# Decoder layer: score groups paired, the router's chain in later slots, and the scan's output broadcast by DMA

## The chip, the cores and the metric

The kernel runs on one core of one Trainium2 chip. The metric is the device time of one execution in microseconds, the median of repeated runs; lower is better. TensorE's clock is granted by the chip at 2.4 GHz (1.00 in the profile) or at half of it, 1.2 GHz (0.50).

## The reference

A decoder layer on 16 batches of 256 tokens with 256 dimensions, in float32, with three parts, each followed by a residual and a layer norm (`d`, `ctx` and the weights are inputs):

```
xh, gate = split(x @ W_in.T + b_in)               # 512 + 512
xh = silu(conv4(xh) + conv_b)
u  = xh @ W_ssm.T + b_ssm                         # 32 states
h_t = h_{t-1} @ A.T + u_t * Bv ; s_t = h_t @ Cv   # scan over the tokens: one number s per token
y  = (s + Dv) * xh * silu(gate)
x  = norm(x + (y @ W_out.T + b_out + x))
x  = norm(x + attention(q=x, k=v=ctx))            # 16 heads of 16
x  = norm(x + moe(x))                             # router softmax, best of 8 experts, 640 places each
```

The last layer norm and the expert sum run over 4096 tokens; a token beyond an expert's 640 places is passed through, so the router must count the tokens in order.

## The kernel before

`decoder` runs three blocks one after the other. `mixer_in` (L63) projects all tokens, convolves, and computes the scan as a few matmuls with precomputed powers of A; it leaves `gated` = xh * silu(gate) for all tokens in SBUF and the scan's output `s_all` (L370), [128 partitions x 64], in a folded layout. `attend` (L375) does everything from the mixer's output to the router for one batch after the other. `experts` (L1058) runs the eight experts.

`attend` is a software pipeline written out by hand. `run` (L455) calls `step(n, p)` of each engine for n from -1 to 19, the middle ones in a hardware loop. A step has 16 slots h. In step n the engines work on several batches at once: the mixer's output of batch n+1, the keys and queries of batch n, the first scores and the values of n-1, the second scores of n-2 and n-3, the output projection of n-3, the router of n-4. Each engine goes through its own step in program order and waits on semaphores; a wait holds all that stands behind it on that engine. The rows call a stretch of one step a batch here, from one first score group to the next.

TensorE (`step`, L780). `scores` (L702) forms query by key of one pair of heads with four matmuls of 48 rows, two on the lower and two on the upper half of the array (L711), into `ps_m`; VectorE takes the row maxima from there (L946), and the next group waits for that. After all eight groups `maxima_rows` (L695, L699) transposes the maxima, ScalarE copies them (`mrow`, L857), and SyncE sends them into `qst`. `scores_t` (L715, L721) forms key by query with the maxima subtracted, into `ps_a`; ScalarE takes the exponential into `pt` (L903), and the next group waits for that. `weigh` (L725, L736) multiplies four heads with the values. There is one buffer of `ps_m` and one of `ps_a`. `scores` stands in even slots, `scores_t` AL = 3 slots behind, so in odd ones.

The dense matmuls take turns on one PSUM bank `ps_d`: `spread_s` (slot 12, L644), `mixer_out` (14 and 15, L670), `keys` (1 and 2), the transposes of `x1` (5), `queries` (7, L689), `values` (9 and 10). The bank `ps_e` goes round among `maxima_rows` (0), the transposes of `pay` (1), `router` (2), `count` (6), `sums_by_query` (7 and 9, L741), the transposes of `onrm` (11), `project_out` (12 and 13, L751).

How s gets to y before the change: VectorE lays s of one batch on the diagonal of `diag` (slot 7, L1044), `spread_s` multiplies it with a matrix of ones, which leaves s of all 256 tokens on all 128 partitions in `ps_d`, and VectorE forms `y` = (s + Dv) * gated from PSUM (slot 13, L1050).

VectorE (`step`, L937), slots: 0: row maximum, `r1` (L951, the residual of the mixer from `ps_d`), `pay` (L959, the norm after attention of batch n-4), the statistics of `r1`; 1: mean and variance, `ve1`; 2: statistics of `pay`; 3: `x1` (L977), `ve3`, the logits `lg` (L986) and their maximum; 4: the negated maximum `ntop` (L994), the index, the one-hot rows `hot` (L1000); 6 to 9: place in the expert, `dest`; 8 and 10: `onrm` (L1029); 14: `r2` (L1035, the residual of attention from `ps_e`) and its statistics; 15: `ve2`.

ScalarE (L851): the exponentials, the copies out of PSUM, `kq` with bias (slots 3 and 8), the high halves of keys and queries (`half`, slots 4 and 9). GpSimd (POOL, L587): powers for the norms, the low halves (L583), `twice` (L609), `x2b` and the scatter of the rows. SyncE (L526) stores the halves to DRAM and reads them back stacked into `kst` and `qst` (`store`, `stack`, L500): keys and queries of batch n must be back before the first scores of step n+1. Its queue is one order too.

## Time and profile before

| | |
|---|---|
| median of 3 runs | 1017.29 us (1015.42 to 1017.44) |
| the profiled execution | 1020.84 us, its span 1019.1 us |
| busy over the span | TensorE 85%, its weight loads 65%, VectorE 59%, ScalarE 40%, GpSimd 35% |
| mean granted clock | 0.909 |
| `mixer_in` / `attend` / `experts` begin at | 0 / 141.0 / 739.1 us |
| row maximum (L946), exponential (L903), mean of 128 | 1.224, 1.025 us |
| memset of `kst` on GpSimd, from 141.18 (L568) | 7.24 us |
| issue of one transfer on SyncE (at 142.19) | 0.38 us |

The profile is one execution; its own time is 3.55 us over the median. A row of a timeline gives the start, the duration of a run of like instructions, engine, line, operation and tiles, their number, and in brackets the idle time of the engine before it and what ended that. Starts of successive rows are the safer measure, since the ends of matmuls are modelled and overlap.

### The profile page before, as it was taken

The page shows a single profiled execution, that of the slowest core. Times are in us where ns is not written, and L with a number is a line of the kernel's source. Part 1 is how long each engine was busy: PE and PEld are TensorE (multiplying, and loading weights), DVE is VectorE, ACT ScalarE, POOL GpSimd, SP SyncE. Part 2 cuts the span into 40 slices and gives each one's busy share as a digit, 9 for nine tenths or more (in the row PEclk, how much of TensorE's full clock was granted, in tenths as well). Part 3 has the DMA queues.
Part 4 walks back from the last instruction along what each step waited for, and adds up shares of the span by engine and source line. Part 5 has one row for each costly group of instructions (what it writes and reads, how often), then busy time and mean ns, then how long its engine had stood idle before and what let it go on. Part 6 is the DMA issues. An engine that isn't in the chain of part 4 may idle for free. (4 is left out here: it accounts for less than half of the span.)

```text
span 1019.1 us, 16854 instructions
## 1 busy us (share of the span) xinstructions
PE 863.1 (85%) x5964; PEld 663.5 (65%) x5964; DVE 597.7 (59%) x1441; ACT 405.0 (40%) x623; POOL 354.1 (35%) x290
## 2 busy tenths in 40 slices
PE   5998947789899888988989888887279999999993
PEld 4776725455666566655666556544279999999993
DVE  4889751545675777667676666643235555555542
ACT  4565611145444444445444454443043334233320
POOL 0333352222233434344342443223212442244422
PEclk9999967679998999999999998877579999999997
DMA  3117302444443445444344442400343222343100
GB/s 115 42 43 210 108 24 78 113 106 126 104 126 115 109 111 125 124 113 114 103 124 121 117 114 74 116 21 24 106 135 109 94 88 90 113 128 106 46 22 22
DMA packets 73432, 98.82 MB, mean 97 GB/s; under 512 B 10529, under 2 KB 60874, under 8 KB 73376
## 3 DMA queue, kind: packets, MB, share of 16 engines
q1 hardware_dynamic: 69920, 89.95, 32.0%
q0 software_dynamic: 3456, 8.13, 2.2%
q8 instruction: 34, 0.56, 0.2%
q14 instruction: 22, 0.18, 0.1%
HBM read 63.40 MB, written 35.73 MB: 97 GB/s over the span
## 5 line engine op out<-in xcount | busy, mean ns | idle before, releaser
L946 DVE TENSOR_REDUCE nmax<-ps_m 128x4 f32<-128x1024 f32 x128 | 156.6, 1224 | 174.6 <-PE ps_m L711 172.1
L903 ACT ACTIVATE pt<-ps_a 128x1024 f32<-128x1024 f32 x128 | 131.1, 1025 | 89.7 <-PE ps_a L721 88.3
L1216 ACT ACTIVATE hid<-ps_h 128x640 fp32r<-128x640 f32 x64 | 45.1, 705 | 151.3 <-PE ps_h L1156 151.3
L1156 PE MATMUL ps_h<-xt,w_hi 128*128 128x320 f32 x512 | 99.9, 318 | 1.0 <-DVE xt L1231 1.0
L1168 PE MATMUL ps_y<-w_hi,hid 128*128 128x256 f32 x640 | 85.3, 284 | 1.7 <-issue 1.7
L1265 DVE SCALAR_TENSOR_TENSOR hid<-ps_h,hid 128x640 fp32r<-128x640 f32 x64 | 52.7, 824 | 56.2 <-ACT hid L1216 55.7
L1156 PEld LDWEIGHTS ps_h<-xt,w_hi 128*128 128x128 f32 x512 | 80.0, 191 | 5.5 <-DVE hid L1265 3.9
L1168 PEld LDWEIGHTS ps_y<-w_hi,hid 128*128 128x128 f32 x640 | 80.1, 192 | 1.9 <-issue 1.9
L721 PE MATMUL ps_a<-qst,kst 49*128 49x256 f32 x512 | 67.8, 345 | 15.5 <-ACT pt L903 15.2
L721 PEld LDWEIGHTS ps_a<-qst,kst 49*128 49x128 f32 x512 | 40.8, 197 | 57.0 <-issue 31.8
L711 PE MATMUL ps_m<-kst,qst 48*128 48x256 f32 x512 | 66.9, 342 | 11.1 <-DVE nmax L946 5.9
L736 PE MATMUL ps_o<-pt,vals 128*32 128x256 f32 x1024 | 74.6, 412 | 0.0
L340 DVE SCALAR_TENSOR_TENSOR conv<-ps_xh,taps,conv 128x510 f32<-128x510 f32 (+2 forms) x96 | 71.7, 747 | 3.4
L158 POOL TENSOR_TENSOR gated<-xh,sgate 128x512 f32<-128x512 f32 x32 | 42.3, 1320 | 90.3 <-ACT xh L245 90.3
L674 PE MATMUL ps_d<-w_out_sb,y 128*128 128x256 f32 x256 | 66.8, 409 | 5.2 <-DVE y L1050 5.2
L1312 POOL DMA_INDIRECT out_rows<-gated,token x40 | 39.4, 985 | 84.1 <-issue 84.1
L711 PEld LDWEIGHTS ps_m<-kst,qst 48*128 48x128 f32 x512 | 41.5, 200 | 39.9 <-issue 23.1
L583 POOL TENSOR_TENSOR half<-kq,half 128x512 fp32r<-128x512 f32 x32 | 40.6, 1268 | 73.0 <-ACT half L841 73.0
L674 PEld LDWEIGHTS ps_d<-w_out_sb,y 128*128 128x128 f32 x256 | 49.0, 201 | 16.3 <-DVE y L1050 6.7
L1156 PE MATMUL ps_h<-xt,w_lo 128*128 128x320 f32 x256 | 58.9, 312 | 0.0
L1279 DVE SCALAR_TENSOR_TENSOR gated<-ps_y,gated 128x256 f32<-128x256 f32 x40 | 19.3, 483 | 64.8 <-PE ps_y L1168 64.8
L1300 POOL TENSOR_TENSOR w_lo<-gated,w_hi 128x2048 fp32r<-128x2048 f32 x8 | 47.4, 5923 | 27.1 <-ACT w_hi L1206 27.1
(169 smaller groups left out, 1654.9 us busy)
## 6 DMA issues: line engine op xcount, KB each, us to landing
halves_dram<-half SPq DMA_DIRECT2D x64, 256.0 KB, 2.4
gated<-in_w SPq DMA_DIRECT2D x16, 1024.0 KB, 5.4
kst<-halves_dram SPq DMA_DIRECT2D x64, 128.0 KB, 3.1
qst<-halves_dram SPq DMA_DIRECT2D x64, 128.0 KB, 3.2
rows_dram<-blank SPq DMA_DIRECT2D x1, 5160.0 KB, 19.7
gated<-rows_dram SPq DMA_DIRECT2D x8, 645.0 KB, 4.2
x_raw<-in_x_t SPq DMA_DIRECT2D x8, 512.0 KB, 3.9
xres<-in_x SPq DMA_DIRECT2D x16, 256.0 KB, 3.6
```

What stands on the lines that cost most here:

```text
L340: op = nc.vector.scalar_tensor_tensor(out[:, :, late:S], ps[:, :, 0:S - late], taps[:, m, k:k + 1], out[:, :, late:S], ALU.mult, ALU.add)
L674: mm = pe.matmul(ps_d[:, t * D:(t + 1) * D], y[:, m, t * P:(t + 1) * P], w["out"][:, m, :], start=(m == 0), stop=(m == MH - 1), skip_group ...
L711: mm = pe.matmul(ps_m[:, side, t, :], qst[base:base + MR, p, k, t * P:(t + 1) * P], kst[base:base + MR, p, k, :], start=True, stop=True, s ...
L721: mm = pe.matmul(ps_a[:, side, t, :], kst[base:base + MR + 1, p, k, t * P:(t + 1) * P], qst[base:base + MR + 1, p, k, :], start=True, stop ...
L736: mm = pe.matmul(ps_o[VW * i:VW * (i + 1), g, :], vals[:, p, t, h, :], pt[:, h // 2 % 4, h % 2, t, :], start=(t == 0), stop=(t == KT - 1), ...
L903: nc.scalar.activation(pt[:, k % 4].rearrange("p s t q -> p (s t q)"), ps_a[:].rearrange("p s t q -> p (s t q)"), ACT.Exp).then_inc(s["exp ...
L946: nc.vector.tensor_reduce(nmax[:, q, :, :, h // 2].rearrange("p t s -> p s t"), ps_m[:], AX.X, ALU.max, negate=True).then_inc(s["max_done" ...
L1156: mm = pe.matmul(ps_h[:, f % 2, c2, 0:HC], w1[a][:, p, k, f * P:(f + 1) * P], xt[:, b, p, k, c2 * HC:(c2 + 1) * HC], start=(n == 0 and k = ...
L1168: mm = pe.matmul(ps_y[:, (p + t) % 2, 0:D], hid[:, a, f, t * P:(t + 1) * P], w2[b][:, p, f, :], start=(n == 0 and f == 0), stop=(n == 2 an ...
L1216: nc.scalar.activation(hid[:, HI, f, :].rearrange("p (c n) -> p c n", c=2), ps_h[:, f % 2, :, 0:HC], ACT.Relu).then_inc(s["hid_hi"], 1)
L1265: nc.vector.scalar_tensor_tensor(hid[:, LO, f, :].rearrange("p (c n) -> p c n", c=2), ps_h[:, f % 2, :, 0:HC], 0.0, hid[:, HI, f, :].rearr ...
L1300: nc.gpsimd.tensor_tensor(flat(w2[LO][:, p]), flat(w2_raw), flat(w2[HI][:, p]).bitcast(F32), ALU.subtract).then_inc(s["w2_lo"], 1)
```

## The change

Five things. `AL` goes from 3 to 4, so that a group of `scores` and a group of `scores_t` stand one behind the other in each even slot, and the other work of TensorE follows them; `weigh` moves ahead of the dense work of its slot. The dense work gets new slots: `mixer_out` 11 and 13, `values` 8 and 9, `sums_by_query` 8 and 10, the transposes of `onrm` 12, `project_out` both halves in 14. The router's chain moves back: transposes of `pay` 2, `router` 4, `lg` to `hot` 5, `count` 7, the rest a slot later; the statistics of `r1` come before `pay`, `r2` goes to slot 15, and `ntop` is made by ScalarE. `diag`, `spread_s` and the mask go: at the end of `mixer_in` TensorE transposes `s_all`, VectorE copies it, and SyncE writes it in four transfers to DRAM; `load_s` reads one batch's 256 numbers repeated over 128 partitions into `sb`, two batches ahead, and `y` (slot 6) is formed from it. The waits for `v_out` and `q_out` that stood in `spread_s` stand in `mixer_out`. Declarations of tiles and semaphores are left out here.

```diff
@@ -147,6 +149,12 @@
             sp.dma_start(dram["rows"].rearrange("(t p) r -> p t r", p=P),
                          c["blank"][:, None, :].to_broadcast([P, E * CAP // P, ROW])).then_inc(c["rows_blank"], 16)
 
+            sp.wait_ge(st_ready, 1)
+            for cq in range(4):
+                sp.dma_start(dram["scan"].rearrange("b (q c i) -> q b c i", q=4, c=4)[cq],
+                             c["s_rows"][B * cq:B * (cq + 1), :].rearrange("p (c n) -> p c n", c=4)[:, :, 0:L]
+                             ).then_inc(c["scan_out"], 16)
+
         @block.gpsimd
         def _(pool):
@@ -226,6 +234,12 @@
                                ends[:, 0:4 - lag, :].rearrange("p c b -> p (c b)"),
                                start=False, stop=(lag == 3), skip_group_check=True)
             mm.then_inc(s_mm, 1)
+
+            pe.wait_ge(s_ready, 1)
+            pe.wait_ge(gate_ready, MH * NG)
+            pe.wait_ge(c["loaded"], 16 * len(c["loads"]))
+            pe.transpose(ps_gate[0:4 * B, 0, 0:P], s_all[:].rearrange("p c b -> p (c b)"), c["eye"][:]
+                         ).then_inc(st_mm, 1)
 
         @block.scalar
@@ -368,7 +382,9 @@
             last.then_inc(ends_ready, 1)
             dve.wait_ge(s_mm, 1)
             nc.vector.tensor_copy(s_all[:], ps_xh[:, 0, 0:4 * B].rearrange("p (c b) -> p c b", b=B)).then_inc(s_ready, 1)
-            dve.wait_ge(s_ready, 1)
+            dve.wait_ge(st_mm, 1)
+            nc.vector.tensor_copy(c["s_rows"][:], ps_gate[0:4 * B, 0, 0:P]).then_inc(st_ready, 1)
+            dve.wait_ge(st_ready, 1)
@@ -381,22 +397,22 @@
...
-    AL, WL = 3, 5
+    AL, WL = 4, 5
@@ -496,6 +513,11 @@
...
+
+            def load_s(j, p):
+                settled(sp)
+                need(sp, s["y_done"], j - 1)
+                sp.dma_start(sb[:, p], dram["scan"][bass.ds(j, 1), :].to_broadcast([P, S])).then_inc(s_in[p], 16)
...
+            sp.wait_ge(c["scan_out"], 64)
+            load_s(0, 0)
             load_x(0, 0)
             load_ctx(0, 0)
 
             def step(n, p):
+                if on(n, -2):
+                    load_s(n + 2, p)
@@ -641,13 +667,6 @@
...
-            def spread_s(j):
-                pe.wait_ge(s["diag_done"], j + 1)
-                need(pe, s["v_out"], j - 1)
-                need(pe, s["q_out"], j)
-                pe.matmul(ps_d[:, 0:S], ones[:], diag[:].rearrange("p c i -> p (c i)"), start=True, stop=True
-                          ).then_inc(s["sbc_mm"], 1)
@@ -670,6 +689,8 @@
             def mixer_out(j, t):
                 if t == 0:
                     pe.wait_ge(s["y_done"], j + 1)
+                    need(pe, s["v_out"], j - 1)
+                    need(pe, s["q_out"], j)
@@ -782,45 +803,46 @@
                 for h in range(NH):
                     if h % 2 == 0 and on(n, 1):
                         scores(n - 1, q, h // 2)
-                    if h == 0 and on(n, 2):
-                        maxima_rows(n - 2, p)
                     j, head, lag = behind(n, h, AL)
                     if head % 2 == 0 and on(n, lag):
                         scores_t(j, p if lag == 2 else q, head // 2)
-                    if h == 12 and on(n, -1):
-                        spread_s(n + 1)
-                    if h in (14, 15) and on(n, -1):
-                        mixer_out(n + 1, h - 14)
-                    if h in (1, 2) and on(n, 0):
-                        keys(n, p, h - 1)
+                    if h == 0 and on(n, 2):
+                        maxima_rows(n - 2, p)
+                    j, head, lag = behind(n, h, WL)
+                    if head % PV == PV - 1 and on(n, lag):
+                        weigh(j, p if lag == 2 else q, head // PV)
+                    if h == 1 and on(n, 0):
+                        keys(n, p, 0)
+                    if h == 2 and on(n, 4):
+                        pe.wait_ge(s["x2_done"], n - 3)
+                        if on(n, 2):
+                            pe.wait_ge(s["m_out"], n - 1)
+                        turn(ps_e, pay[:, p], s["x2t_mm"])
+                    if h == 2 and on(n, 0):
+                        keys(n, p, 1)
+                    if h == 4 and on(n, 4):
+                        router(n - 4)
                     if h == 5 and on(n, 0):
                         pe.wait_ge(s["k_out"], n + 1)
                         pe.wait_ge(s["x1_done"], n + 1)
                         turn(ps_d, x1, s["x1t_mm"])
+                    if h == 7 and on(n, 4):
+                        count(n - 4)
                     if h == 7 and on(n, 0):
                         queries(n, 0)
                         queries(n, 1)
-                    if h in (9, 10) and on(n, 1):
-                        values(n - 1, q, h - 9, n if on(n, 0) else None)
-                    if h == 6 and on(n, 4):
-                        count(n - 4)
-                    if h in (7, 9) and on(n, 3):
-                        sums_by_query(n - 3, (h - 7) // 2)
-                    if h == 11 and on(n, 3):
+                    if h in (8, 10) and on(n, 3):
+                        sums_by_query(n - 3, (h - 8) // 2)
+                    if h in (8, 9) and on(n, 1):
+                        values(n - 1, q, h - 8, n if on(n, 0) else None)
+                    if h == 12 and on(n, 3):
                         pe.wait_ge(s["on_done"], 2 * (n - 3) + 2)
                         turn(ps_e, onrm, s["ont_mm"])
-                    if h in (12, 13) and on(n, 3):
-                        project_out(n - 3, h - 12)
-                    if h == 1 and on(n, 4):
-                        pe.wait_ge(s["x2_done"], n - 3)
-                        if on(n, 2):
-                            pe.wait_ge(s["m_out"], n - 1)
-                        turn(ps_e, pay[:, p], s["x2t_mm"])
-                    if h == 2 and on(n, 4):
-                        router(n - 4)
-                    j, head, lag = behind(n, h, WL)
-                    if head % PV == PV - 1 and on(n, lag):
-                        weigh(j, p if lag == 2 else q, head // PV)
+                    if h in (11, 13) and on(n, -1):
+                        mixer_out(n + 1, (h - 11) // 2)
+                    if h == 14 and on(n, 3):
+                        project_out(n - 3, 0)
+                        project_out(n - 3, 1)
@@ -859,7 +881,13 @@
...
-                    if h == 5 and on(n, 4):
+                    if h == 6 and on(n, 0):
+                        act.wait_ge(s["x1t_mm"], n + 1)
+                        nc.scalar.copy(x1t[:].rearrange("p k t -> p (k t)"), ps_d[:]).then_inc(s["x1t_out"], 1)
+                    if h == 6 and on(n, 4):
+                        act.wait_ge(s["top_out"], n - 3)
+                        nc.scalar.mul(ntop[:], top[:, :, 0], -1.0).then_inc(s["ntop_out"], 1)
+                    if h == 7 and on(n, 4):
                         j = n - 4
                         act.wait_ge(s["ntop_out"], j + 1)
                         need(act, s["pay_ready"], j)
...
-                    if h == 6 and on(n, 0):
-                        act.wait_ge(s["x1t_mm"], n + 1)
-                        nc.scalar.copy(x1t[:].rearrange("p k t -> p (k t)"), ps_d[:]).then_inc(s["x1t_out"], 1)
...
-                    if h == 12 and on(n, 3):
+                    if h == 13 and on(n, 3):
...
-                    if h == 11 and on(n, 1):
+                    if h == 10 and on(n, 1):
...
-                    if h == 2 and on(n, 4):
-                        act.wait_ge(s["x2t_mm"], n - 3)
-                        nc.scalar.copy(x2t[:].rearrange("p k t -> p (k t)"), ps_e[:]).then_inc(s["x2t_out"], 1)
...
+                    if h == 2 and on(n, 4):
+                        act.wait_ge(s["x2t_mm"], n - 3)
+                        nc.scalar.copy(x2t[:].rearrange("p k t -> p (k t)"), ps_e[:]).then_inc(s["x2t_out"], 1)
@@ -951,7 +976,13 @@
...
-                    if h == 0 and on(n, 4):
+                    if h == 0 and on(n, 0):
+                        dve.wait_ge(s["r1_done"], n + 1)
+                        stats(st1, r1, s["stats1"])
+                    if h == 1 and on(n, 0):
+                        mean_var(dc, st1, mv1, s["stats1"], n)
+                        nc.vector.tensor_scalar(ve1[:], mv1[:, :, 1], EPS, None, ALU.add).then_inc(s["var1_ready"], 1)
+                    if h == 1 and on(n, 4):
                         dve.wait_ge(s["rstd2"], i + 1)
...
-                    if h == 0 and on(n, 0):
-                        dve.wait_ge(s["r1_done"], n + 1)
-                        stats(st1, r1, s["stats1"])
-                    if h == 1 and on(n, 0):
-                        mean_var(dc, st1, mv1, s["stats1"], n)
-                        nc.vector.tensor_scalar(ve1[:], mv1[:, :, 1], EPS, None, ALU.add).then_inc(s["var1_ready"], 1)
...
-                    if h == 3 and on(n, 4):
+                    if h == 5 and on(n, 4):
+                        need(dve, s["ntop_out"], i)
                         dve.wait_ge(s["logit_mm"], i + 1)
                         nc.vector.tensor_copy(lg[:].rearrange("p t e -> p (t e)"), ps_e[:, 0:KT * E]).then_inc(s["lg_out"], 1)
                         dve.wait_ge(s["vo_row"], 1)
...
-                    if h == 4 and on(n, 4):
+                    if h == 5 and on(n, 4):
+                        dve.wait_ge(s["vo_row"], 1)
                         dve.wait_ge(s["top_out"], i + 1)
-                        nc.vector.tensor_scalar(ntop[:], top[:, :, 0], -1.0, None, ALU.mult).then_inc(s["ntop_out"], 1)
...
-                    if h == 6 and on(n, 4):
...
-                    if h == 7 and on(n, 4):
...
-                    if h == 8 and on(n, 4):
...
-                    if h == 9 and on(n, 4):
...
-                    if h in (8, 10) and on(n, 3):
-                        t = (h - 8) // 2
+                    if h in (9, 11) and on(n, 3):
+                        t = (h - 9) // 2
...
-                    if h == 14 and on(n, 3):
+                    if h == 15 and on(n, 3):
...
-                    if h == 7 and on(n, -1):
-                        need(dve, s["sbc_mm"], n + 1)
-                        nc.vector.tensor_tensor(diag[:], s_all[:, :, bass.ds(n + 1, 1)].to_broadcast([P, 4, 64]),
-                                                mask[:, None, :].to_broadcast([P, 4, 64]), ALU.mult
-                                                ).then_inc(s["diag_done"], 1)
-                    if h == 13 and on(n, -1):
-                        dve.wait_ge(s["sbc_mm"], n + 2)
+                    if h == 6 and on(n, -1):
+                        dve.wait_ge(s_in[q], use(n + 1, 16, q))
+                        need(dve, s["wout_mm"], n + 1)
                         for m in range(MH):
-                            op = nc.vector.scalar_tensor_tensor(y[:, m, :], ps_d[:, 0:S], c["d_col"][:, m:m + 1],
+                            op = nc.vector.scalar_tensor_tensor(y[:, m, :], sb[:, q], c["d_col"][:, m:m + 1],
                                                                 gated[:, m, bass.ds((n + 1) * S, S)], ALU.add, ALU.mult)
                         op.then_inc(s["y_done"], 1)
```

## Rows read from the trace of the kernel before

**Rows 1.** Busy times by stretch: length, five engines' busy, PEclk, DMA share, GB/s.

```profile
264.21:617.20 352.99, 317.83 (x2346) 215.56 (x2344) 241.57 (x649) 165.46 (x275) 142.81 (x132) 0.96 0.43 115
...
296.60:329.98 33.38, 30.28 (x216) 20.71 (x214) 21.64 (x59) 15.02 (x25) 12.99 (x12) 0.90 0.40 112
...
362.56:393.52 30.96, 27.66 (x215) 18.73 (x213) 22.16 (x59) 15.06 (x25) 12.96 (x12) 1.00 0.45 120
393.52:425.43 31.91, 29.04 (x216) 19.72 (x214) 21.47 (x59) 15.05 (x25) 12.95 (x12) 0.95 0.45 116
```

**Rows 2.** Waits of TensorE from 264.21 to 616.9: us in total, times, longest.

```profile
PE ps_e L774 <- DVE hot L1000: 11.9, 11, 1.3
PE ps_a L721 <- ACT pt L903: 10.0, 11, 1.0
```

**Rows 3.** The same columns as rows 1, a stretch at half clock.

```profile
341.90:345.30 3.40, 3.40 (x12) 2.68 (x9) 0.56 (x3) 1.07 (x2) 0.64 (x1) 0.50 0.02 6
```

**Rows 4.** Timeline of TensorE in the batch from 362.56.

```profile
362.56 0.39 PE L699 MATMUL ps_e<-eye,nmax 128*16 128x128 f32 x2
...
364.64 1.10 PE L656 MATMUL ps_d<-ctx,w_k_sb 128*128 128x256 f32 x4 [0.26 <-DVE r L951]
...
368.40 0.50 PE L721 MATMUL ps_a<-qst,kst 49*128 49x256 f32 x4
368.74 0.40 PE L711 MATMUL ps_m<-kst,qst 48*128 48x256 f32 x4
369.06 1.07 PE L736 MATMUL ps_o<-pt,vals 128*32 128x256 f32 x16
370.10 0.50 PE L721 MATMUL ps_a<-qst,kst 49*128 49x256 f32 x4
370.53 0.66 PE L682 MATMUL ps_d<-eye,x 128*128 128x128 f32 x4
...
374.56 1.99 PE L689 MATMUL ps_d<-x1t,w_q_sb 128*128 128x256 f32 x8
...
384.38 0.70 PE L648 MATMUL ps_d<-diag,ones_sb 128*128 128x256 f32 x2
384.92 1.03 PE L755 MATMUL ps_e<-w_o_sb,ont 128*128 128x256 f32 x4
```

**Rows 5.** Timeline of VectorE in the same batch.

```profile
363.82 0.68 DVE L951 TENSOR_TENSOR r<-ps_d,x2b 128x512 f32<-128x512 f32 x1
...
369.44 0.17 DVE L986 COPY lg<-ps_e 128x16 f32<-128x16 f32 x1
...
369.87 1.21 DVE L946 TENSOR_REDUCE nmax<-ps_m 128x4 f32<-128x1024 f32 x1
370.99 0.94 DVE L994 TENSOR_SCALAR ntop<-top 128x2 f32<-128x2 f32 x1
...
372.44 0.36 DVE L1000 TENSOR_SCALAR hot<-kinds_sb,expert 128x8 bf16<-128x8 f32 x2
...
390.06 0.68 DVE L1035 TENSOR_TENSOR r<-ps_e,gated 128x512 f32<-128x512 f32 x1
...
391.91 0.17 DVE L1041 TENSOR_SCALAR ve<-mv 128x2 f32<-128x2 f32 x1
```

**Rows 6.** Timeline of TensorE in an early batch, where the transfers are waited for.

```profile
220.94 2.71 PE L689 MATMUL ps_d<-x1t,w_q_sb 128*128 128x256 f32 x8
...
236.54 0.50 PE L711 MATMUL ps_m<-kst,qst 48*128 48x256 f32 x4 [0.47 <-DMA qst<-halves_dram]
```

**Rows 7.** Timeline of POOL and of VectorE in the batch of rows 4.

```profile
372.74 2.44 POOL L609 TENSOR_SCALAR twice<-pay,mv,ve 128x256 f32<-128x256 f32 x2 [0.18 <-POOL ve L605]
...
374.68 0.43 DVE L1044 TENSOR_TENSOR diag<-s_all,mask_sb 128x256 f32<-128x256 f32 x1
```

**Rows 8.** Timeline of all engines as attention begins.

```profile
149.03 1.00 DVE L1044 TENSOR_TENSOR diag<-s_all,mask_sb 128x256 f32<-128x256 f32 x1
...
151.41 1.66 DVE L1050 SCALAR_TENSOR_TENSOR y<-ps_d,d_col_sb,gated 128x256 f32<-128x256 f32 x4 [1.38 <-PE ps_d L648]
```

28 lines of the change are left out of this document (16 added, 12 removed).

## The prediction

> **What bounds the kernel now.** I began with the table of time and profile: TensorE is busy 85% of the span, VectorE 59%, so I looked for the stretch where TensorE's order sets the pace. That is the middle stage, attention with the mixer's output and the router riding along. The view by stretches [rows 1] shows 11 alike batches in 352.99 us, 32.09 each. Three of the 11 run wholly at the granted clock of 1.00 (2.4 GHz) and take about 30.96, of which TensorE is busy 27.66 and idle 3.30. The other eight hold a spell at 1.2 GHz (mean 0.95, once 0.90) and take 31.9 to 33.4 [rows 1]. The waits of TensorE over the same batches [rows 2] say where the idle time comes from: the router's chain on VectorE (`hot`, 11.9 us in 11 batches), and right behind it the exponential on ScalarE (10.0). The spell at 1.2 GHz starts just after these two waits: one is seen at 341.9 [rows 3].
>
> The timeline of TensorE [rows 4] gives prices. A score group alone holds the engine from 370.10 to 370.53, 0.43 us. Two groups back to back hold it from 368.40 to 369.06, 0.66, not 0.86: a saving of 0.20 a pair. `spread_s` holds it 0.53 (384.38 to 384.92).
>
> **What the change does to a batch.** I walk from T, the start of the first score group, at full clock.
>
> Removed. `spread_s`: -0.53. Pairing: 16 groups stood in 15 places (one pair exists, the one just read), now in 8: 7 new pairs at 0.20, -1.40. On VectorE `diag` (0.43) and the negated maximum go; the latter was held 0.94 at 370.99 [rows 5] behind a POOL operation, though its work is small. On ScalarE the same negation comes in, a small instruction before an exponential that has not yet been asked for: nothing, or 0.3 if that cover is gone. Of the old 3.30 idle I take all out and put in the new waits:
>
> (1) The residual `r2` now runs in slot 15, after both halves of `project_out`, which end with the batch. TensorE's maxima transposes wait for it: 0.68 of DVE [rows 5], 0.12 to start and 0.14 to hand over (`r1` ends at 364.50, the keys start at 364.64 [rows 4, 5]) make T+0.94, against a pair that ends at T+0.66. New wait 0.28.
>
> (2) The keys wait for `r1`. On VectorE `r2` to `ve2` takes 390.06 to 392.08, 2.02; then the max reduce, 1.14 to the next start; then `r1`, 0.68 [rows 5]. Before, the `r2` chain ran under the last matmuls. Now it starts only after them, so the keys start at T + 0.12 + 2.02 + 1.14 + 0.68 + 0.14 = T+4.10. TensorE has until then a pair, the maxima (0.39 with its tail, 0.32 net) and a weigh group (1.00 net) [rows 4], and is free at T+2.26. New wait 1.84, the largest one, in place of 0.26. Moving `mixer_out` forward to slots 11 and 13 does not help: its sum has long been there when VectorE is free to read it.
>
> (3) The normalised rows `pay` now stand after `stats1` and `ve1`. Their transposes wait about 0.15 more; if POOL's power on `ve1` holds VectorE off, up to 0.85.
>
> (4) The router's logits are read after the third reduce. From `r1` to `lg` was 5.62 [rows 5]; with a reduce ahead of it T+3.28+5.62+1.14 = T+10.0, and the router itself ends at T+10.2 by TensorE's order. From `lg` to `hot` took 3.36, of which the reduce was 1.12 (369.87 to 370.99) and the held negation 0.94 less 0.09 of overlap [rows 5]: 1.39 left, so `hot` is ready at T+11.6 and the count starts at T+11.75. TensorE comes there at T+11.45 with nothing late. Wait 0.3, or 0.6 with one small operation held; I take 0.45.
>
> The waits of the later slots (`onrm`, `ont`) go: between each producer and its reader there is now a `mixer_out` half (1.9) or the values. Full-clock batch: 30.96 - 0.53 - 1.40 - 3.30 + (0.28 + 1.84 + 0.15 + 0.45) = 28.45 us.
>
> **The queries' way through DRAM.** The next batch's first scores wait for transfers that start with the queries. In an early batch the chain was bare: the queries end at 223.65, the scores start at 236.54 on their arrival, 12.9 us [rows 6]. The change puts one exponential (1.02, in the table) between the bias and the high half: 13.9. The queries end at T+13.9 (count 0.2, queries 1.99 [rows 4]), so the data land at T+27.8, 0.7 before TensorE. If they are late by up to 1.6 the keys' wait of (2) absorbs it. SyncE's queue gets a scan load at the head of a step, 0.4 of issue where it idles. Price 0.
>
> **The clock.** What the old waits cost in clock is 32.09 - 30.96 = 1.13 a batch, 1.0 to 1.7 in a batch that has a spell. The new waits (1) and (2) are 2.1 us of idleness with 1.3 of work between them; the old pair, 11.9 + 10.0 over 11 batches [rows 2], was 2.0 with 0.2 of work between. I expect a spell in nearly every batch and take 1.5, so 29.95. Per batch -2.1, over 11 batches -23.
>
> **`y` from SBUF.** `y` now reads two SBUF tensors and falls beside POOL's `twice`. In the rows `diag`, which also reads two, took 0.43 inside `twice` (374.68 in 372.74 to 375.18), but 1.00 beside a POOL operation with two inputs at 149.03 [rows 7, 8]. I take 0, since the neighbour is `twice`; bounds 0 to 1.2, half of `twice`. The Trainium skill ("SBUF — State Buffer", section Who interferes with whom) says that a VectorE instruction with two SBUF inputs contends with any GpSimd instruction that reads SBUF and that the later one fully blocks. By that rule `diag` at 374.68 would have waited and `y` would wait: the trace agrees at 149.03 and not at 374.68.
>
> **The edges.** Before attention: a transpose, a copy, four transfers. If all engines wait for the four issues (0.38 each, in the table) the stage starts 1.7 to 2.3 later, with POOL's memset of 7.24 (in the table) on the path; against it `diag` and `spread_s` no longer stand between 149.03 and `y` at 151.41 [rows 8]: -2.4. Sum 0, bounds -2 to +3. The scan's own way through DRAM hides under the memset. The batch before the 11 gains some 2, the first with exponentials may lose 1, the last steps without keys gain 1 and the drain loses 1, where the last weigh group is now ahead of the router. Together -1.
>
> **Sum:** -23 - 1 = -24 on the profiled execution's 1020.84, 996.8; that execution stands 3.55 over the median of the runs shown, so the forecast is 993.
>
> **Rivals.**
> A, the clock holds: the wait (2) is one piece, and in three batches of eleven waits of this size cost no clock. Then 28.45 a batch, -3.64 x 11 = -40, with the edges -41: 976. Against: the new wait is as long as the old two. Chance 0.12.
> B, half the gain or less: reduce and exponential of the groups before now both stand in front of one place, the second group of a pair sometimes waits, and pairing saves 0.7, not 1.4; (3) and (4) take their upper ends, 0.85 more. Then 28.45 + 1.55 + 1.5 = 31.5, -0.6 a batch, -7 with the edges: 1010. Against: at 368.40 a pair ran without a wait. Chance 0.12.
> C, `y` is held by `twice` each batch: `sums_by_query` waits for the place behind it, 0.6 to 1.2 on 11 batches: 1000 to 1006. Chance 0.08, since `diag` ran through. The rule of the Trainium skill on "SBUF — State Buffer", named above, makes this the outcome.
> D, slower: the clock stays at 1.2 GHz from the keys' wait through the keys, turn and router, because every wait there feeds the next. The 28.45 batch becomes the old 32.09 when 3.6 us are lost to the clock, that is 7.3 us at 1.2 GHz, a mean of 0.89. In one batch 0.90 is seen. With 10 us it is 33.5: +15, 1032. Chance 0.06.
> E, the two sides cancel, within 0.2% of before: 0.04.
> The forecast, 984 to 1001, keeps 0.58. A measurement of this kernel tells about 0.2% (2 us) from no change. Faster is forecast, A, B and C: 0.90; same 0.04; slower 0.06. The range 976 to 1010 reaches to A and to B and takes in C and the upper ends of (3), (4) and the prologue.
>
> **What would show it.** In the profile after: batches of 29.5 to 30.5; a wait of the keys on `r1` near 1.8 as TensorE's largest, one of the maxima on `r2` of 0.3, that on `hot` under 0.6, those on `onrm` gone; adjacent L711 and L721 groups at 0.66; `r2` directly after `project_out`. Wrong if the keys wait under 0.5, if the first scores wait for DMA over 1.6, if the mean clock of the batches is under 0.90 or all at 1.00.

## The result, and the profile after

| | before | after |
|---|---|---|
| median, us | 1016.36 (4 runs) | 975.67 (4 runs, 973.87 to 978.80) |
| ratio | | 0.9611, 95% interval 0.9571 to 0.9652 |
| profiled execution, us (span) | 1020.84 (1019.1) | 973.87 (972.1) |
| granted clock, 11 batches | 0.96 | 0.98 |

The change takes 3.9% off. (Ratios, here and below, leave disturbed runs out, so one can differ from the quotient of two medians, most for the first set with statistics in front, where two of four runs are left out.) 975.67 is 17 us under the forecast of 993 and 0.3 under the low end of the range. Taken as a ratio, so that the kernel before of the same set counts, it lies just inside: 976 on 1017.29 is 0.959, and 0.961 was measured. The medians differ by 40.7 us and the two profiled executions by 47.0, since the one of before is 4.5 over its median and the one after 1.8 under; 6.3 us of the table below are of that kind. It divides up the 47.0 (a batch begins with its maxima transposes, L699 before and L720 after):

| stretch | before | after |
|---|---|---|
| mixer, up to `s_all` | 140.29 | 137.46 |
| start of attention, first batches | 67.61 | 68.39 |
| the next two | 29.08, 27.23 | 29.85, 28.20 |
| the 11 alike batches | 352.99 | 316.09 |
| the last two steps | 30.75, 28.52 | 27.71, 23.83 |
| drain | 62.61 | 62.97 |
| experts | 280.0 | 277.6 |

So 36.9 of the 47.0 us lie in the 11 batches. This is the view by stretches of the kernel after, for all 11, for one batch at full clock and for one with a spell at 1.2 GHz, in the columns of [rows 1]:

```profile
263.90:579.99 316.09, 279.90 (x2321) 197.93 (x2321) 238.60 (x633) 164.46 (x286) 144.70 (x132) 0.98 0.49 132
...
292.78:320.34 27.56, 24.90 (x213) 17.60 (x211) 20.68 (x56) 14.99 (x26) 13.02 (x12) 1.00 0.46 135
320.34:350.16 29.82, 26.43 (x213) 18.71 (x212) 22.01 (x58) 14.99 (x26) 13.11 (x12) 0.94 0.46 129
```

A batch takes 28.74 on average. TensorE's work at full clock is about 24.85, its idle time (316.09 - 279.90) / 11 = 3.29, and the rest, 0.60, is work done at the lower clock. Before it was 27.66 + 3.20 + 1.23 = 32.09. Of the 3.35 us that a batch gains, 2.81 are therefore work that TensorE no longer does and 0.63 work that it no longer does at the lower clock; it waits as long as before. Four of the 11 batches hold a spell, where it was eight of 11 [rows 1].

The waits of TensorE over these batches of the kernel after (us in total, times, longest):

```profile
PE ps_d L675 <- DVE r L976: 16.0, 11, 2.0
PE ps_m L732 <- DMA qst<-halves_dram: 8.3, 11, 1.5
PE ps_e L795 <- DVE hot L1026: 8.0, 11, 0.9
PE ps_e L703 <- DVE pay L990: 2.6, 9, 0.4
PE ps_m L732 <- DVE nmax L971: 1.0, 3, 0.3
PE ps_e L720 <- DVE r L1061: 0.2, 1, 0.2
```

The waits for the exponential of [rows 2] and for `onrm` are gone, and that for `hot` fell from 11.9 to 8.0. The largest is now the keys' wait for `r1`. One that I had priced at nothing, the first scores' wait for their transfers, comes second.

The timeline of TensorE of the kernel after, across the edge of a batch:

```profile
349.49 0.51 PE L732 MATMUL ps_m<-kst,qst 48*128 48x256 f32 x4 [0.55 <-DMA qst<-halves_dram]
349.83 0.40 PE L742 MATMUL ps_a<-qst,kst 49*128 49x256 f32 x4
350.16 0.39 PE L720 MATMUL ps_e<-eye,nmax 128*16 128x128 f32 x2
350.48 1.07 PE L757 MATMUL ps_o<-pt,vals 128*32 128x256 f32 x16
353.03 1.10 PE L675 MATMUL ps_d<-ctx,w_k_sb 128*128 128x256 f32 x4 [1.48 <-DVE r L976]
...
355.03 0.66 PE L703 MATMUL ps_e<-eye,pay 128*128 128x128 f32 x4 [0.23 <-DVE pay L990]
...
360.97 0.18 PE L795 MATMUL ps_e<-hot,tri 128*128 128x8 bf16 x1 [0.60 <-DVE hot L1026]
...
365.18 1.89 PE L684 MATMUL ps_d<-w_v_sb,ctx 128*128 128x256 f32 x8
367.00 0.50 PE L732 MATMUL ps_m<-kst,qst 48*128 48x256 f32 x4
```

And the timeline of VectorE of the kernel after in the same batch, with one row of POOL (at 361.04) that stands beside `y`:

```profile
349.09 0.69 DVE L1061 TENSOR_TENSOR r<-ps_e,gated 128x512 f32<-128x512 f32 x1 [1.04 <-PE ps_e L776]
349.82 0.75 DVE L952 BATCH_NORM_STATS2 st<-r 128x6 f32<-128x256 f32 x2
...
351.06 1.23 DVE L971 TENSOR_REDUCE nmax<-ps_m 128x4 f32<-128x1024 f32 x1
352.20 0.68 DVE L976 TENSOR_TENSOR r<-ps_d,x2b 128x512 f32<-128x512 f32 x1
...
359.32 0.17 DVE L1012 COPY lg<-ps_e 128x16 f32<-128x16 f32 x1 [0.34 <-PE ps_e L785]
...
360.55 0.36 DVE L1026 TENSOR_SCALAR hot<-kinds_sb,expert 128x8 bf16<-128x8 f32 x2
...
361.04 2.69 POOL L635 TENSOR_SCALAR twice<-pay,mv,ve 128x256 f32<-128x256 f32 x2 [0.18 <-POOL ve L631]
...
362.25 1.89 DVE L1072 SCALAR_TENSOR_TENSOR y<-sb,d_col_sb,gated 128x256 f32<-128x256 f32 x4
...
365.53 1.22 DVE L1041 TENSOR_SCALAR over<-place 128x2 f32<-128x2 f32 x1
```

Read the two together. From T = 349.49 the pair takes until 350.16, 0.67 as forecast. The keys start at T+3.54, not T+4.10: `r2` already began at T-0.40, since it waits for the projection and not for the scores, while the scores themselves were held 0.55 by the transfer. From `r2` at 349.09 to `hot` at 360.55 VectorE has one gap above 0.2 us, the 0.34 ahead of `lg`. In that stretch TensorE waits three times (1.48, 0.23, 0.60).

### The profile page after: what moved, and what is told of

Its sections match the earlier page's. It is cut to its first block and busy times, and to the rows that moved or that the text cites. A ratio compares the mean times of both kernels' runs of the same rounds, so it can differ in the third digit from the quotient of the medians.

```text
span 972.1 us, 16867 instructions
## 1 busy us (share of the span) xinstructions
PE 805.2 (83%) x5933; PEld 635.1 (65%) x5933; DVE 594.3 (61%) x1410; ACT 404.9 (42%) x639; POOL 356.3 (37%) x290
## 5 line engine op out<-in xcount | busy, mean ns | idle before, releaser
L695 PE MATMUL ps_d<-w_out_sb,y 128*128 128x256 f32 x256 | 62.1, 388 | 11.1 <-DVE y L1072 9.8
L675 PE MATMUL ps_d<-ctx,w_k_sb 128*128 128x256 f32 x128 | 42.6, 466 | 21.1 <-DVE r L976 21.1
L646 POOL DMA_INDIRECT rows_dram<-pay,dest x32 | 33.2, 1036 | 64.0 <-DVE dest L1047 50.0
```

What stands on the lines that cost most here:

```text
L675: mm = pe.matmul(ps_d[:, m * S:(m + 1) * S], w["k"][:, k, m * P:(m + 1) * P], ctx[:, p, k, :], start=(k == 0), stop=(k == KD - 1), skip_gr ...
L695: mm = pe.matmul(ps_d[:, t * D:(t + 1) * D], y[:, m, t * P:(t + 1) * P], w["out"][:, m, :], start=(m == 0), stop=(m == MH - 1), skip_group ...
```

## The experiments

Times are medians, beside runs of the kernel before on the same chip. "Batches" is the same stretch of 11 in the profiled execution, and "TensorE idle" its idle time there. One execution can lie off its median: pairing alone was profiled at 999.01 us (7.3 over), all but the pairing at 984.33 (4.3 under), the early projection at 956.19 (5.8 under), the wait on `sel` at 955.85 (4.6 over).

| kernel | time | ratio to before (95%) | batches | TensorE idle |
|---|---|---|---|---|
| before | | | 352.99 | 35.2 |
| scan alone | 1015.30 | 1.0006 (0.9984 to 1.0027) | 352.59 | 37.7 |
| pairing alone | 991.73 | 0.9744 (0.9722 to 0.9767) | 333.81 | 29.9 |
| all but the pairing | 988.66 | 0.9729 (0.9713 to 0.9745) | 323.65 | 25.1 |
| the change | 975.67 | 0.9611 (0.9571 to 0.9652) | 316.09 | 36.2 |
| statistics in slot 12 | 976.82 | 0.9615 (0.9587 to 0.9642) | 317.27 | 36.1 |
| statistics in front, first set | 988.89 | 0.9659 (0.9574 to 0.9744) | 328.78 | 40.9 |
| statistics in front, second set | 983.15 | 0.9668 (0.9624 to 0.9713) | 321.66 | 40.6 |
| r1 first | 979.07 | 0.9636 (0.9603 to 0.9669) | 317.16 | 35.8 |
| q's split first | 976.90 | 0.9622 (0.9573 to 0.9671) | 322.21 | 32.5 |
| early projection | 961.96 | 0.9479 (0.9436 to 0.9521) | 301.00 | 22.1 |
| both of these | 954.96 | 0.9404 (0.9373 to 0.9435) | 299.85 | 19.4 |
| and a late count | 953.82 | 0.9377 (0.9340 to 0.9414) | 300.51 | 24.6 |
| and a wait on `sel` | 951.25 | 0.9298 (0.9254 to 0.9341) | 292.63 | 16.1 |

### The parts of the change by themselves

**Pairing alone**, on the kernel before:

```diff
-    AL, WL = 3, 5
+    AL, WL = 4, 5
```

> The kernel before with AL = 4 and nothing else: the two score groups share an even slot, all other work keeps its old slot. Theory S (a change between score groups and full-array matmuls costs TensorE some 0.1 us each way, and seven fewer of both make about 2 us less busy time a batch): TensorE's busy time per batch falls from 27.7 to about 25.7 to 26.3 at full clock, and some of it comes back as longer waits for hot, whose chain on VectorE has not moved: 10 to 22 us faster. Theory W (the gain came from the waits that the new slots took away and from the clock that they cost): busy time falls by at most 1.4 a batch and the waits take nearly all of it: within 5 us of before.

**All of the change but the pairing**, on the kernel after:

```diff
-    AL, WL = 4, 5
+    AL, WL = 3, 5
```

> The changed kernel with AL = 3: all new slots, the transfers for the scan, but score groups in alternate slots again. Theory S: 2 us more TensorE time in each of some 13 batches, partly under the waits for r1: 18 to 30 us slower than the changed kernel. Theory W: under 10 us slower.

**The scan by transfers alone**, on the kernel before, with `y` in its old slot and the slots of the router and projections as they were:

```diff
-            def spread_s(j):
...
+            def load_s(j, p):
+                settled(sp)
+                need(sp, s["y_done"], j - 1)
+                sp.dma_start(sb[:, p], dram["scan"][bass.ds(j, 1), :].to_broadcast([P, S])).then_inc(s_in[p], 16)
...
-                            op = nc.vector.scalar_tensor_tensor(y[:, m, :], ps_d[:, 0:S], c["d_col"][:, m:m + 1],
+                            op = nc.vector.scalar_tensor_tensor(y[:, m, :], sb[:, q], c["d_col"][:, m:m + 1],
```

> The kernel before with the scan's output repeated by transfers alone; diag and spread_s go, y is formed in slot 13 from sb, all else in its old slot. Both theories: 0.53 us of TensorE and 0.43 of VectorE less in 16 batches, and 1.5 to 2.5 us more before attention begins: 3 to 7 us faster. If the transfers for it disturb those of the scores, no gain or a loss.

What was measured: the view by stretches, of each kernel one batch that ran wholly at the full clock (of pairing alone the only one). First pairing alone:

```profile
442.75:471.48 28.73, 26.15 (x215) 18.45 (x214) 22.46 (x59) 15.03 (x25) 13.00 (x12) 1.00 0.50 129
```

All but the pairing:

```profile
355.57:384.34 28.77, 26.69 (x211) 17.99 (x211) 21.09 (x58) 14.90 (x27) 13.22 (x12) 1.00 0.50 134
```

The scan alone:

```profile
486.81:517.64 30.83, 27.29 (x213) 18.34 (x211) 22.20 (x58) 15.05 (x25) 12.94 (x12) 1.00 0.48 124
```

The second number is TensorE's work, 27.66 before. Pairing takes off 27.66 - 26.15 = 1.51 in the old order, and 26.69 - 24.85 = 1.84 in the new one. The scan takes off 0.37. All but the pairing takes off 0.97, so by difference the new slots bring some 0.6 of work, where I had none. The scan alone leaves the time as it was, where both theories had it 3 to 7 us faster: its idle time grows from 35.2 to 37.7, which is the 0.37 x 11 put back in two thirds (the copy `ont`, 2.7 in 11 batches, is waited for once `spread_s` no longer stands in front of its reader).

In time, pairing is worth 24 alone and 13 on top of the slots; the slots with the scan are worth 27 alone and about 16 on top of the pairing. Theory W falls on the kernel before, where the work fell by more than its 1.4 and the time by far more than its 5 us; theory S has the work right (26.15) and the time 2 to 4 us short. On top of the slots neither range holds: 13 lies between the "under 10" of W and the 18 to 30 of S. The two halves do not add up, since together they run into waits: idle time is 29.9 with the one, 25.1 with the other, and 36.2 with both. Against all but the pairing, the change waits 8.0 for `hot` where that kernel waits 0.8, and 8.3 for the load of the scores where that kernel has none; the keys' wait is nearly the same in both (16.0 and 15.5).

### What the front of the batch is bound by

**r1 first**: the statistics of `r2` and their mean move from the end of slot 15 to behind `r1`, on VectorE.

```diff
+                    if h == 0 and on(n, 4):
+                        dve.wait_ge(s["r2_done"], i + 1)
+                        stats(st2, c["r2"], s["stats2"])
...
                     if h == 15 and on(n, 3):
...
-                        dve.wait_ge(s["r2_done"], j + 1)
-                        stats(st2, c["r2"], s["stats2"])
```

> The changed kernel with the statistics of r2 (stats2, mean_var, ve2) moved behind r1 on VectorE, so that the keys wait no longer for them. Theory K (the chain project_out, r2, statistics, reduce, r1, keys sets the batch): the keys' wait falls from 1.45 to some 0.3, the batch from 28.7 to about 27.4: 12 to 16 us faster. Theory Q (the transfers that start with the queries and end at the next first scores are a second bound of nearly the same length, as the wait of 0.75 for them hints): the batch is a loop through keys, queries and transfers, and since the keys start earlier the transfers do as well: also faster, with the DMA wait larger than 0.75. If instead the wait for r1 was free because of the transfers: within 3 us of the changed kernel.

The waits of TensorE in that kernel:

```profile
PE ps_e L703 <- DVE pay L997: 14.4, 11, 1.4
PE ps_m L732 <- DMA qst<-halves_dram: 8.5, 11, 1.1
...
PE ps_d L675 <- DVE r L976: 4.5, 11, 0.5
```

The keys' wait fell from 16.0 to 4.5, that for `pay` rose from 2.6 to 14.4, and the batches stayed (317.16 for 316.09). The load's wait did not move either. Theories K and Q are wrong by their 12 to 16 us; the third reading has the time nearly right (within 3 us; 3.4 measured, with intervals that overlap) but not its reason, the transfers. The theory that describes it, called V from here: whichever instruction of TensorE's is in front, it meets VectorE's stretch from `r2` to `hot`; moving one instruction inside the stretch only moves the wait.

**Two more statistics per batch**, of a constant, into a tile that nobody reads: once behind `r1`'s own statistics in the stretch, once in slot 12.

```diff
+                        for t in range(KT):
+                            nc.vector.bn_stats(st_x[:, t, :], c["b_o"][:, 0:D])
```

> The changed kernel with two more batch statistics per batch on VectorE, of a constant, into a tile that nobody reads, put right behind the statistics of r1 (slot 0). By the rows of the changed kernel such a pair takes about 0.7 us. Theory V (the first third of a batch is VectorE's: its instructions run back to back from r2's drain to hot, and TensorE's waits there are that one stretch seen at several places): each of the 11 batches is longer by about 0.7, TensorE's waits for keys, pay and hot grow by that sum, and the time is 982 to 985 us. Rival M (the stretch of VectorE merely lies beside TensorE's, and the wait for the scores' load at the batch's edge takes up what comes late): below 3 us, 975 to 978 us.

> The same two statistics per batch, but in slot 12, where VectorE is idle. It adds the same work to VectorE's busy sum (about 0.7 us a batch), and the instruction order elsewhere is unchanged. Theory V: within 1 us of the changed kernel, 974 to 977 us, since only what lies between r2's drain and hot counts. Rival W (VectorE's total of work is what matters, wherever it stands): the same loss as with the statistics in front, 982 to 985 us.

> The kernel with the two extra statistics in front, once more: its four times lay between 974.76 and 992.29, too far apart to read a price from. In its profiled execution TensorE idled 41.1 us over the 11 batches (36.9 in the changed kernel) and the lower clock took 7 us more than in the kernel with the statistics in slot 12. Theory: the 0.7 us of VectorE costs 4 to 5 us by itself, and the rest is the clock, which differs from one execution to the next, so that the times spread from 978 to 993 with a median of 983 to 990 us. Rival: the four times were an accident and the median is 975 to 979 us.

In slot 12 they cost nothing: 976.82. In front they make it 988.89 (974.76 to 992.29) in the first set and 983.15 (977.00 to 989.00) in the second. By the ratios to before that is 0.4 to 0.5% more than in slot 12, 4.5 to 5.5 us, for 0.74 x 11 = 8 us of VectorE. The intervals of the first set are too wide to tell it, and that of the second still overlaps the one of slot 12 a little, so the times alone do not settle it. The idle time of TensorE says the same in both sets: 40.9 and 40.6 with the work in front, 36.1 with it in slot 12, 36.2 without it (the third text above has 36.9 for the last). The waits of the second set's profiled execution:

```profile
PE ps_d L676 <- DVE r L977: 14.7, 11, 1.7
PE ps_m L733 <- DMA qst<-halves_dram: 10.3, 11, 2.1
PE ps_e L704 <- DVE pay L993: 7.8, 11, 0.8
```

`pay`, the next reader behind the extra work, is waited for 7.8 - 2.6 = 5.2 us longer. As far as this tells, the totals of VectorE do not matter (rival W falls), the place of its work does.

**q's split first**: ScalarE splits q's high half ahead of the exponentials of slot 8.

```diff
-                    if h == 9 and on(n, 0):
-                        split_hi(n, s["q_out"], s["q_hi"], s["k_stored"], 32 * n + 32)
...
                         add_bias(bq, s["q_out"])
+                        split_hi(n, s["q_out"], s["q_hi"], s["k_stored"], 32 * n + 32)
```

> The changed kernel, where only the order on ScalarE of slot 8 is altered: q's high half is split before the exponentials instead of after them, so that q's store and the reload for the first scores of the next batch start about a microsecond earlier. The projection stays in its late place. TensorE waits 0.75 us a batch for that load now. Theory V (the load's wait lies ahead of VectorE's stretch from r2 to hot and is taken back by it: what TensorE gains there it waits at the keys): the load's wait goes and the keys' and maxima's waits grow by as much; within 3 us of the changed kernel, 973 to 977 us. Rival Q (the load closes the batch's cycle): 8 to 11 us less, 965 to 968 us.

The load's wait fell by 5.8 us, from 8.3 to 2.5, and those for `r1` (16.0 before) and `r2` (0.2) took up 4.3 of it:

```profile
PE ps_d L675 <- DVE r L975: 18.5, 11, 2.1
...
PE ps_m L732 <- DMA qst<-halves_dram: 2.5, 4, 1.3
PE ps_e L720 <- DVE r L1060: 2.0, 7, 0.3
```

The time is unchanged, 976.90, as V has it; rival Q's 965 to 968 did not come. In all TensorE idled 3.7 us less, and in the profiled execution the clock of the batches was 0.94, so that it is not to be seen. The load does not close the cycle.

### Taking work out of the stretch

**Early projection**: both halves of `project_out` in slot 13, `mixer_out`'s second half behind them in 14, the transposes of `onrm` ahead of the weigh group of slot 12, `ont` copied in 12, `r2` and its statistics on VectorE in slot 13. Its mean and `ve2` stay in slot 15; in the profiled execution `ve2` ended 0.14 us behind the start of the next first scores (342.61), in the changed kernel 1.64 behind. The lines that move `onrm`, `ont` and `r2` are left out here.

```diff
-                    if h in (11, 13) and on(n, -1):
-                        mixer_out(n + 1, (h - 11) // 2)
-                    if h == 14 and on(n, 3):
+                    if h in (11, 14) and on(n, -1):
+                        mixer_out(n + 1, (h - 11) // 3)
+                    if h == 13 and on(n, 3):
```

> The changed kernel with the projection of onrm moved before the second half of mixer_out: ont is copied in slot 12, both halves of the projection stand in slot 13, the last half of mixer_out in slot 14, and r2's drain with its statistics in slot 13, so that r2 and its statistics run while TensorE does mixer_out. Theory V: some 2.2 us of VectorE's work (r2 0.8, statistics and means 1.4) leave the stretch at the batch's start; TensorE's wait for keys falls from 1.45 to below 0.5 us a batch and the time by 8 to 14 us, to 961 to 968 us; the wait for the scores' load at the batch's edge, 0.75 now, is what stands next and may grow. Rival K (the front is set by PSUM or by the load, not by VectorE): keys' wait goes and comes back in full at the first scores or at hot, 973 to 978 us.

> As the one before (projection ahead of mixer_out's second half), and with ScalarE splitting q's high half before the exponentials of slot 8, so that its store and the reload of the next scores start about a microsecond earlier. Theory V with the load as next bound: the wait at the first scores gets shorter by up to what it had grown, and the time lies another 2 to 7 us below that of the kernel with the early projection alone, 955 to 964 us. Rival: if the load is not what bounds after the projection is moved, the two kernels agree within 2 us.

The waits of the early projection alone:

```profile
PE ps_e L795 <- DVE hot L1026: 7.8, 11, 0.9
PE ps_m L732 <- DMA qst<-halves_dram: 5.7, 11, 0.9
PE ps_d L675 <- DVE r L976: 4.6, 11, 0.5
```

The keys' wait is 0.42 a batch, as V has it, and did not come back elsewhere. The time falls by 13.7 us to 961.96, which is 0.9479 of before. With q's split first as well it is 954.96: the step that brought nothing on the changed kernel brings 7 us here by the medians, at the edge of what the intervals can tell (0.9436 and 0.9435). The profiled executions show less of it. The load's wait is gone (5.7 before), TensorE idles 2.7 us less, the batches fall by 1.15 and the execution by 2.1, from one that lay 5.8 under its median. That VectorE's stretch no longer takes the load's wait back fits this; the 7 us are not shown to come from it. By the view by stretches, that kernel's batch from 341.22 takes 26.53 for 25.03 of work:

```profile
341.22:367.75 26.53, 25.03 (x214) 17.63 (x212) 20.71 (x57) 14.88 (x26) 13.12 (x13) 1.00 0.49 139
```

**Late count**: the count's matmuls behind the queries.

```diff
-                    if h == 7 and on(n, 4):
-                        count(n - 4)
                     if h == 7 and on(n, 0):
                         queries(n, 0)
                         queries(n, 1)
+                    if h == 7 and on(n, 4):
+                        count(n - 4)
```

> The kernel with the early projection and the early split of q, and with the count's matmuls behind the queries of slot 7 instead of ahead of them (queries need x1t only, which is ready). TensorE waits 0.71 us a batch for hot there (7.8 over 11). Theory H (each microsecond of wait in TensorE's order is a microsecond of the batch, and a little more through the clock): the wait for hot is gone, nothing replaces it, since sel's drain on VectorE stands behind y, which ends later anyway, and the time is 6 to 11 us below 954.96, 944 to 949 us. Rival D (with that wait gone the reload of the scores or VectorE's chain from the queries' maxima is late by as much): the first scores wait again by 0.5 to 0.7 us a batch and the time is 952 to 956 us.

The wait for `hot` (7.8 us) went, and a new one came, in a place that neither theory had (the time lies in rival D's 952 to 956, but the first scores wait only 1.1 us for their load). The waits of TensorE:

```profile
PE ps_e L769 <- DVE carry L1032: 11.6, 10, 1.3
PE ps_d L675 <- DVE r L975: 4.8, 11, 0.5
```

The attention sums' transposes wait for `carry`, a sum of 128x8 bf16. Its row in one batch, and the row of POOL beside it:

```profile
353.65 1.19 DVE L1032 TENSOR_TENSOR carry<-carry,hot 128x8 bf16<-128x8 bf16 x1
```

```profile
353.56 1.26 POOL L609 TENSOR_TENSOR half<-kq,half 128x512 fp32r<-128x512 f32 x1 [0.31 <-ACT half L863]
```

It is held for as long as POOL's operation runs; in the changed kernel, where it fell between two POOL operations, the same sum took 0.14. All 11 batches ran at the full clock here, but the time, 953.82, is within 1.2 us of the kernel without the late count: one wait took the place of the other.

**The transposes wait for `sel`**, whose read is what frees the PSUM bank, and no longer for `carry`:

```diff
-                    need(pe, s["place_done"], j)
+                    need(pe, s["sel_out"], j)
```

> The kernel with the late count, where TensorE's transposes of the attention sums wait for sel, which is what frees the PSUM bank, and no longer for the carry addition behind it. In the late-count kernel that addition took 1.19 us instead of the 0.14 it takes elsewhere: it began at 353.65, 0.09 after POOL's two-input operation half of 1.26 us, and TensorE waited 1.33 for it. Theory N (a small VectorE instruction with two SBUF inputs is held until a POOL two-input instruction is over): the carry addition still takes 1.2 us but nobody waits for it; sel ends at 353.7, TensorE's wait there falls from 1.16 a batch to 0.1 to 0.3, and the time is 8 to 11 us below 953.82, 943 to 946 us. Rival G (what was gained in front is bounded by another closed chain: the exponentials' copies of the sums, the scores' reload or VectorE's next statistics): the wait appears again at the first scores or at onrm, and the time is 951 to 954 us.

`carry` still takes up to 1.21, and nobody waits for it; the same transposes wait 1.7 us for `sel`, in 11 batches. The batches, and one of them, by the view by stretches:

```profile
260.27:552.90 292.63, 276.56 (x2324) 195.86 (x2322) 235.43 (x628) 164.74 (x286) 146.10 (x133) 1.00 0.51 143
339.72:366.14 26.42, 25.15 (x213) 17.79 (x212) 21.24 (x57) 14.90 (x26) 13.14 (x13) 1.00 0.53 143
```

The 11 batches fall by 7.9 us, as theory N says, and TensorE idles 16.1 us for 24.6, so the wait did not come back elsewhere, against rival G. The time falls by only 2.6, to 951.25, which is G's number and not N's. Two things lie between. The kernel before took 1022.54 in this set, against 1018.00 beside the late count; against before the ratio goes from 0.9377 to 0.9298, 8 us, with intervals that just meet. And the profiled execution is 4.6 over its median: what follows the last batch mark took 349.6 us against 339.7 in the kernel with the late count, in code that is the same. The trace shows where. Two of the eight instructions of `experts` that make `w_lo` on VectorE were held beside POOL's own `w_lo`, for 4.8 us each, which is 9.6 of the 9.9. Here is one, and one of the six that were not:

```profile
791.39 7.10 DVE L1256 TENSOR_TENSOR w_lo<-gated,w_hi 128x2048 fp32r<-128x2048 f32 x1
...
827.58 2.27 DVE L1256 TENSOR_TENSOR w_lo<-gated,w_hi 128x2048 fp32r<-128x2048 f32 x1
```

```profile
791.70 4.64 POOL L1321 TENSOR_TENSOR w_lo<-gated,w_hi 128x2048 fp32r<-128x2048 f32 x1
...
828.30 6.04 POOL L1321 TENSOR_TENSOR w_lo<-gated,w_hi 128x2048 fp32r<-128x2048 f32 x1
```

Of the two engines one is held: VectorE in the first pair, POOL by some 1.4 in the second. The profiled execution of pairing alone has one such instruction (6.46 at 839.96) and those of before, of the change and of the late count have none. The kernel with the wait on `sel` is the fastest version, 7.0% under the kernel before and 3% under the change.

## Why the prediction was wrong in size and right in kind

The direction, the stretch and the new largest wait were right. The forecast is 23 us too high on the profiled execution (996.8 for 973.87), in three terms of the batch and one outside it.

| per batch | forecast | measured |
|---|---|---|
| TensorE's work at full clock | 27.66 - 1.93 = 25.73 | 24.85 |
| waits | 2.72 | 3.29 |
| lower clock | 1.50 | 0.60 |
| sum | 29.95 | 28.74 |

**Work, -1.93 forecast, -2.81 measured.** This is the mis-sized term, "7 new pairs at 0.20, -1.40" and what I left beside it at nothing. Pairing is 1.51 in the old order and 1.84 in the new, `spread_s` 0.37 for the 0.53 of its row (its neighbour's start may overlap with it; not shown), and the slots, priced at zero, are 0.6. The rows show how: the values, eight matmuls in one piece at 365.18, hold TensorE until 367.00, 1.82. Before, the same eight ran in two pieces, 1.13 from 378.79 and 1.06 from 381.35 to 382.41:

```profile
378.79 1.13 PE L665 MATMUL ps_d<-w_v_sb,ctx 128*128 128x256 f32 x4
...
381.35 1.13 PE L665 MATMUL ps_d<-w_v_sb,ctx 128*128 128x256 f32 x4
382.41 0.50 PE L721 MATMUL ps_a<-qst,kst 49*128 49x256 f32 x4
```

That is 0.37 of the 0.6. A group that is put beside its like also spares its neighbours something. I had measured the gain of a pair between the two groups only. That the saving is at the borders between score groups (48 or 49 rows) and matmuls on all 128 is argued from these sums; no run changed the number of borders alone.

**Waits, 2.72 forecast, 3.29 measured.** (1) the maxima on `r2`: 0.28 forecast, 0.02 measured, since the scores' load holds TensorE and not VectorE, and `r2` is over by then. (2) the keys: 1.84 forecast, 1.45 measured, as the same 0.4 is taken off. (3) `pay`: 0.15, and 0.24 measured. (4) `hot`: 0.45, and 0.73. What was missing is the load, 0.75 a batch. I had it land 0.7 before TensorE on a batch of 28.45; at 27.5, which the smaller work makes, it is late. But it costs little: the forecast's step that the keys' wait absorbs what is late was right, and the run with q's split first shows it. Keys and load together are 2.2, against 1.84.

**Clock, 1.5 forecast, 0.60 measured.** "I expect a spell in nearly every batch": it was four of 11. The step reasoned from the amount of idle time, and the runs contradict that. Pairing alone idles less (29.9 us in 11 batches) and has a spell in 10 of them; the change idles 36.2 and has four; the late count idles 24.6 and has none, while the kernel before it in the table idles only 19.4 and has three. These are single executions, and that of pairing alone was the slowest of its four, with the lowest clock (0.910, the others 0.912 to 0.920), so the contrast may be smaller in the middle. What the position of the waits has to do with it is not settled. What a spell costs is steady in the changed kernel: a batch with one does 26.4 to 26.6 of work for 24.9, 1.6.

**Edges, -1 forecast, about -10 measured.** 5.2 of it (mixer 2.8, experts 2.4) is in stages that the change leaves nearly as they were. Of the whole 47.0, 6.3 is what the two profiled executions lie off their medians. The first batch mark lay anywhere from 205.4 to 207.9 in kernels nearly alike up to there, so I count this part as the difference between executions; what made it is not shown. The two steps after the 11 batches gain 3.0 and 4.7, since they too are batches with paired scores, which I had at 1; their granted clock was higher too (0.96 and 0.83 for 0.89 and 0.76). The two batches before the 11 were 0.8 and 1.0 longer, where I had the first up to 1 longer and the second some 2 shorter: the second ran at 0.82, for 1.00 before. The start of attention, "sum 0, bounds -2 to +3", was +0.8.

**`y`.** I took 0 with bounds to 1.2, and rival C at 0.08. `y` took 1.89 beside `twice` (2.69 at 361.04) for 1.66 before [rows 8], and was not waited for. At the start it was held:

```profile
148.63 3.13 DVE L1072 SCALAR_TENSOR_TENSOR y<-sb,d_col_sb,gated 128x256 f32<-128x256 f32 x4 [0.20 <-DVE b_o_sb L945]
149.37 1.32 POOL L605 TENSOR_TENSOR x2b<-x2b,xres 128x512 f32<-128x512 f32 x1
```

So what runs on POOL decides: in these rows a TENSOR_TENSOR stops VectorE and a TENSOR_SCALAR barely slows it. Whether it is the second input or the operation is not shown. The Trainium skill ("SBUF — State Buffer", section Who interferes with whom) says that a VectorE instruction with two SBUF inputs contends with a GpSimd instruction that reads SBUF, and that the ports they share are an exclusive lock. The rows at 148.63 and 353.65 agree; the row of `y` at 362.25, beside `twice` from 361.04, does not.

**The rivals.** A gives 976, the measured time, by luck: it had the clock at full in every batch and the work at 25.73. Its batch, 28.45 for the measured 28.74, comes near because the work is 0.88 smaller and waits and clock are 0.57 and 0.60 larger, and the edges, which it had at -1 as well, make up for the rest. B fell: pairing gave more than counted, and groups waited for one in front three times in 11 batches, 1.0 us in all. C fell: `y` took 1.89 and `sums_by_query` did not wait for it. D needed a mean clock of 0.89; it was 0.98. E fell with the 3.9%.

**The signs.** None of those that were to show the forecast wrong came: the keys wait 1.45, the first scores 0.75 for their load, the mean clock is 0.98. Of those that were to show it right, the largest wait, the pairs at 0.67 and `r2` directly behind the projection came; the batches are shorter (28.74 on average, for 29.5 to 30.5), `hot` is waited for 0.73 and not under 0.6, and the maxima hardly wait.

## What to carry to other kernels

Count what a block of matmuls costs from its start to its neighbour's start, with the neighbours that it will have; here the pairs were worth 1.84 where their own rows showed 1.40, and the new order 0.6 more. Where a wait only moves when an instruction ahead of it is moved, look for the stretch of the other engine that runs without a gap, and take work out of that stretch: 2.0 us a batch of VectorE, moved under other matmuls, were worth 14 us, where an earlier load had been worth nothing. Look at what a semaphore really guards, since an instruction that merely stands before it may be held by a third engine. And before a slow stretch is put down to the chip, compare the same instructions in both traces: two of them held 9.6 us here.

## What the runs showed of the hardware that was not expected

- A tiny VectorE instruction is held for the whole of a POOL two-input operation: `over` (128x2, one SBUF input) took 1.22 at 365.53 beside POOL's `half` at 365.46, and 0.17 where it fell outside of one; `carry` (bf16, two inputs) took 1.19 and 0.14. The max reduces, which read PSUM, ran through. A long one with two SBUF inputs, `w_lo` of 128x2048, took 7.10 for 2.27 beside POOL's own `w_lo`; in the other pairs POOL's took 6.0 for 4.6. What decides which of the two is held is not settled.
- The granted clock does not follow the sum of idle time: 10 of 11 batches had a spell at 29.9 us of idleness, four at 36.2, three at 19.4 and none at 24.6.
- How far the times of one kernel spread is not shown to depend on where VectorE's extra work stands. With the two statistics in the stretch six runs lie 12 us apart and with the same two in slot 12 four runs within 2.3, but in the set of the six, the kernel before and q's split first, without the extra work, lie 9.4 and 9.7 us apart too.
